# First network's batch 0 turned and routed inside the last attention steps; linear attention's input turned inside the first network

## What is computed

```python
x = L0_attn_x                                              # (4, 512, 256)
x = _layernorm(x + _L0_attn_ref(x, ...))                   # softmax attention, 16 heads of 128, causal, rope
x = _layernorm(x + _L0_ffn_ref(x, ...))                    # gated network, 688 wide, with routed low-rank terms
x = _layernorm(x + _L1_attn_ref(x, Wq, Wk, Wv, Wo, bo))    # linear attention, 32 heads of 64
x = _layernorm(x + _L1_ffn_ref(x, ...))                    # 64 experts of 176, 6 of them per token, and a shared one
```

## Time and profile before

| | |
|---|---|
| median of 3 runs | 1531.04 us (1530.15 to 1536.18) |
| the profiled execution, its own time | 1537.87 us |
| its span, first to last instruction | 1536.1 us |
| PE busy | 1414.8 us, 92% of the span |
| PE weight loads, DVE, ACT, POOL busy | 73%, 61%, 37%, 36% |
| share of the chain that ended last | PE 80%, DVE 9%, POOL 3%, ACT 2% |
| mean granted TensorE clock | 0.967 |

### The profile page before, as it was taken

How to read it: one execution, slowest core, us unless ns; L and a number is a source line. 1 busy time by engine, 2 the same in 40 slices (tenths; PEclk the granted TensorE clock), 3 DMA queues, 4 the chain that set the end, 5 groups by cost and what they waited for, 6 DMA issues and landing times.

```text
span 1536.1 us, 23836 instructions
## 1 busy us (share of the span) xinstructions
PE 1414.8 (92%) x8106; PEld 1126.1 (73%) x8106; DVE 941.8 (61%) x2170; ACT 569.5 (37%) x1441; POOL 553.4 (36%) x483
## 2 busy tenths in 40 slices
PE   7999999999999999889999799999999999766990
PEld 6777777777777777667776588788788788653650
DVE  4677777777777777744432557566665666655214
ACT  4444444444444444612121243343343333321330
POOL 3555555555555555101012223522522522204223
PEclk9999999999999999989999899999999999878996
DMA  5000000000002000110000020110200003945994
GB/s 175 1 11 1 12 0 10 0 10 0 10 0 71 0 0 1 20 62 1 1 0 1 0 76 8 47 37 15 69 7 14 7 9 85 254 153 165 274 257 123
DMA packets 68221, 76.39 MB, mean 50 GB/s; under 512 B 14205, under 2 KB 55445, under 8 KB 68149
## 3 DMA queue, kind: packets, MB, share of 16 engines
q1 hardware_dynamic: 56789, 58.49, 13.8%
q10 hardware_dynamic: 8288, 12.22, 2.6%
q0 software_dynamic: 3072, 4.72, 1.6%
HBM read 66.22 MB, written 9.21 MB: 49 GB/s over the span
## 4 chain that ended last, share of the span: by engine, by line
PE 80%; DVE 9%; POOL 3%; issue 2%; ACT 2%; DMA 2%; another core or an unknown queue 1%; POOLq 0%; ACTq 0%; DVEq 0%
PE ps L1605 37%; PE ps L1721 9%; PE ps L1706 7%; PE ps L1694 5%; PE ps L1751 4%; PE ps L1842 4%; PE ps L1699 2%; PE ps L2046 2%; PE ps L1917 1%; PE ps L2111 1%; PE ps L1907 1%; DMA sums_dram<-rows 1%; PE ps L2128 1%; PE ps L1723 1%; PE ps L1696 1%
## 5 line engine op out<-in xcount | busy, mean ns | idle before, releaser
L616 POOL TENSOR_TENSOR qk<-q,ksb 128x512 f32<-128x512 f32 x64 | 82.5, 1290 | 304.2 <-ACT q L840 214.1
L755 ACT ACTIVATE probs<-ps,nm 128x128 f32<-128x128 f32 (+3 forms) x256 | 133.8, 525 | 152.4 <-DVE nm L1115 152.4
L1721 PE MATMUL ps<-kT,qT 128*128 128x128 f32 (+3 forms) x512 | 174.6, 450 | 4.4 <-ACT probs L755 3.7
L1039 DVE TENSOR_TENSOR pT_low<-ps,pT 128x384 fp32r<-128x384 f32 (+2 forms) x256 | 99.7, 451 | 122.9 <-ACT pT L698 121.3
L1056 DVE TENSOR_TENSOR prod<-ps,rope_sb 128x1024 f32<-128x1024 f32 x128 | 150.2, 1216 | 6.4 <-PE ps L1605 6.4
L494 POOL TENSOR_TENSOR qT<-prod 64x512 f32<-64x512 f32 x64 | 81.2, 1268 | 170.2 <-DVE prod L1056 131.6
L698 ACT ACTIVATE pT<-ps 128x384 fp32r<-128x384 f32 (+2 forms) x256 | 84.9, 416 | 152.4 <-PE ps L1751 152.4
L1706 PE MATMUL ps<-U,oT 128*128 (+1 forms) x512 | 124.6, 386 | 0.7 <-ACT oT L698 0.7
L494 POOL TENSOR_TENSOR kT<-prod 64x512 f32<-64x512 f32 x64 | 81.4, 1272 | 111.6 <-DVE prod L1056 109.1
L1115 DVE TENSOR_REDUCE nm<-ps 128x1 f32<-128x128 f32 (+3 forms) x256 | 114.0, 484 | 12.1 <-PE ps L1723 12.1
L1165 DVE SCALAR_TENSOR_TENSOR acc<-ps,rinv,acc 128x256 f32<-128x256 f32 x256 | 109.6, 479 | 13.5 <-PE ps L1706 11.9
(11 more groups left out here) (256 smaller groups left out, 2746.4 us busy)
## 6 DMA issues: line engine op xcount, KB each, us to landing
eg<-in_L_ffn_w_gate_dram SPq DMA_DIRECT2D x16, 704.0 KB
eg<-in_L_ffn_w_up_dram SPq DMA_DIRECT2D x16, 704.0 KB
ed<-in_L_ffn_w_down_dram ACTq DMA_DIRECT2D x10, 640.0 KB
ksb<-ks_dram SPq DMA_DIRECT2D x16, 256.0 KB, 3.3
ed<-in_L_ffn_w_down_dram SPq DMA_DIRECT2D x6, 640.0 KB
rows_dram<-rows ACTq DMA_DIRECT2D x4, 640.0 KB, 3.9
acc<-in_L_attn_x_dram SPq DMA_DIRECT2D x4, 512.0 KB
wq_in<-in_L_attn_wq_dram SPq DMA_DIRECT2D x8, 256.0 KB, 2.8
```

The costliest lines, as they stand in the source:

```text
L616: nc.gpsimd.tensor_tensor(qk[:], q3[:], ksb[b % 2][:], ALU.mult).then_inc(qk_ready, 1)
L755: nc.scalar.activation(probs[hh][:, off:off + (i + 1) * P], ps[:, BS + i % 2, 0:(i + 1) * P], ACT.Exp, bias=nm[:, hh, i:i + 1], accum_out= ...
L1039: return nc.vector.tensor_tensor(o, whole, hi.bitcast(F32), ALU.subtract)
L1721: pe.matmul(ps[:, bank, 0:(i + 1) * P], qT[:, hh, b, i * P:(i + 1) * P], kT[:, hh, b, 0:(i + 1) * P], start=True, stop=False)
```

## The change

It does four things.

1. Batch 0 is turned in step 6 of the last pair (banks 2 and 3), its halves are made in the same step, and its router products are issued before the last `pv_and`. ACT's sigmoid and DVE's `route0(0)` come before the last `oT` copy and the last additions. Two groups of base products stand around the last `project_out`.
2. The weight pieces are split in another order: `la` third instead of last, so ACT waits for `la` in step 5 instead of step 6, and DVE makes the last three pieces in step 7.
3. In the last batch of the first network batches 0, 1 and 2 of linear attention's input are turned and split (banks 4 and 5): one after tile `m == 3`, one after the last tile, one inside the down products. `x2T` becomes one pair of buffers per batch, `wk3` a first chunk and the later three, and POOL splits the first key weights and centres the values when the last `turn_x1` is done.
4. At the seam the first four key tiles and the first queries come directly after the last products; the statistics, normalisation, turning and splitting of batch 3 come after or beside them, and the bias is added after that.

```diff
-        w0_pieces += [([h[:] for h in lb], lb_in[:]), ([h[:] for h in la], la_in[:])]
+        w0_pieces.insert(2, ([h[:] for h in la], la_in[:]))
+        w0_pieces.append(([h[:] for h in lb], lb_in[:]))
+        w0_hi_at = {4: (0, 1), 5: (2, 3, 4), 6: (5,)}
+        w0_lo_at = {5: (0, 1), 6: (2,), 7: (3, 4, 5)}
...
@@ gpsimd @@
-            pool.wait_ge(ffn_ready, TILES)
-            halve_wk3(0, lambda: root(8))
-            x2_rest(3)
-            pool.wait_ge(x2_ready, TILES)
+            pool.wait_ge(x1_turned, BATCH * KD)
+            halve_wk3(0)
+            centre_wv3(0)
+            root(8)
+            pool.wait_ge(ffn_ready, TILES)
             nc.gpsimd.memset(kvT[0][:].bitcast(F32), 0.0).then_inc(zeroed, 1)
             nc.gpsimd.memset(kvT[1][:].bitcast(F32), 0.0).then_inc(zeroed, 1)
+            x2_rest(3)
...
@@ scalar @@
+                if n == 5:
+                    act.wait_ge(la_loaded, 8 * 16)
                 if n == 6:
                     act.wait_ge(lb_loaded, 64)
-                    act.wait_ge(la_loaded, 8 * 16)
...
+                if last and n == 6:
+                    x1_halves(0)
...
-            x1_halves(0)
             scores0(0)
+            act.wait_ge(pv_done, STEPS * PAIRS)
+            copy(oT[:], ps[:, BO, :]).then_inc(ot_copied, 1)
             xa_halves(0)
...
             for p in range(PPC):
                 keys(0, p, FIRST_KEYS[p])
             grams(0, 0)
+            x2_rows(3)
+            x2_halves(3, 4)
             act.wait_ge(zeroed, 5)
...
@@ vector @@
-                    if n >= 5:
-                        for m in (2 * (n - 5), 2 * (n - 5) + 1):
+                    if n == 6:
+                        x1_rests(0)
+                    if n in w0_lo_at:
+                        for m in w0_lo_at[n]:
...
-            dve.wait_ge(acc_added, 4 * STEPS * PAIRS)
             link(nc.vector.memset(wnext[:], 1.0 / R0))
-            dve.wait_ge(x1_ready, TPB)
-            x1_rests(0)
             route0(0)
             take_weights()
+            add(STEPS * PAIRS - 1, STEPS - 1)
             xa_rests(0)
+            dve.wait_ge(acc_added, 4 * STEPS * PAIRS)
...
             for p in range(PPC):
                 keys(0, p, FIRST_KEYS[p])
+            statistics(tiles(3), 2 * BATCH)
+            norm2(3)
+            x2_rests(3, 4)

             dve.wait_ge(dn_loaded, 13 * 16)
             dve.wait_ge(x2lo_ready, BATCH)
...
@@ tensor @@
+                if n == 6 and last_pair:
+                    pe.wait_ge(products_ready, 2 * PROJECTIONS)
+                    turn_x1(0)
                 for i in range(TPB):
                     pe.wait_ge(probs_ready, 4 * s + i + 1)
...
+                    if m == 3 and last_one:
+                        turn_x2(0, 4)
                 if not last_one:
-                    first_products(b + 1, False)
+                    first_products(b + 1)
+                else:
+                    pe.wait_ge(x2Tlo_ready, KD)
+                    turn_x2(1, 4)
                 pe.wait_ge(hid_ready, b * FT0 + FT0)
                 for i in range(TPB):
+                    if last_one and i == 2:
+                        pe.wait_ge(x2Tlo_ready, 2 * KD)
+                        turn_x2(2, 4)
...
-            turn_x1(0, True)
+            pe.wait_ge(w0_lo, 3)
+            first_products(0)
+            pv_and(STEPS * PAIRS - 1, STEPS - 1)
+            pe.wait_ge(w0_lo, 5)
+            base_products(0, 0, 1)
+            project_out(STEPS * PAIRS - 1, PAIRS - 1, STEPS - 1)
+            base_products(0, 1, 1)
+            turn_xa(0)
             pe.wait_ge(w0_lo, 6)
-            first_products(0, True)
             pe.wait_ge(dn_loaded, 13 * 16)
...
-                               lambda h: wk3[h][:, bass.ds(c, 1), k, :], k == 0, k == KD - 1)
+                               lambda h: wk3_first[h][:, k, :] if at_first else wk3_later[h][:, bass.ds(c - 1, 1), k, :],
+                               k == 0, k == KD - 1)
...
-            pe.wait_ge(ffn_added, TILES)
-            for b in range(BATCH):
-                pe.wait_ge(x2_ready, b * TPB + TPB)
-                for k in range(KD):
-                    for i in range(TPB):
-                        last = pe.transpose(ps[:, 2 * b + k, i * P:(i + 1) * P],
-                                            acc[:, b * TPB + i, k * P:(k + 1) * P], ident[:])
-                    last.then_inc(x2_turned, 1)
-            pe.wait_ge(x2Tlo_ready, BATCH * KD)
             pe.wait_ge(wk3_ready, 1)
+            pe.wait_ge(x2Tlo_ready, 3 * KD)
             for p in range(PPC):
                 keys(0, 0, 0, p, FIRST_KEYS[p])
-            pe.wait_ge(x2lo_ready, BATCH)
-            pe.wait_ge(x2_ones, 2 * BATCH)
+            pe.wait_ge(ffn_added, TILES)
+            pe.wait_ge(wq3_ready, PPC)
+            queries(0, 0, 0)
+            pe.wait_ge(x2lo_ready, 1)
+            pe.wait_ge(x2_ones, 2)
             grams(0, 0)
+            turn_x2(3, 4)
             chunk3(0, True, False)
```

More of the change, by code:

```diff
@@ L737, in ffn_weights_halves, with x1_halves @@
                     act.wait_ge(proj_ready, PROJECTIONS)
+                if n == 5:
+                    act.wait_ge(la_loaded, 8 * 16)
                 if n == 6:
                     act.wait_ge(lb_loaded, 64)
-                    act.wait_ge(la_loaded, 8 * 16)
-                for halves, whole in w0_pieces[2 * (n - 4):2 * (n - 3)]:
+                for m in w0_hi_at[n]:
+                    halves, whole = w0_pieces[m]
                     copy(halves[0], whole).then_inc(w0_hi, 1)
+            def x1_halves(b):
+                for k in range(KD):
+                    act.wait_ge(x1_turned, b * KD + (k + 1))
+                    copy(x1T[b % 2][0][:, k, :], ps[:, x1_bank(b) + k, :]).then_inc(x1hi_ready, 1)
             def step(g, n, first, last):
@@ L822, in ffn0 @@
                         x1_halves(b + 1)
+                    if m == 3 and last:
+                        x2_halves(0, 4)
                 if not last:
@@ L1153, in step, with x1_rests @@
                             rest(halves[1], whole, halves[0]).then_inc(w0_lo, 1)
+            def x1_rests(b):
+                for k in range(KD):
+                    dve.wait_ge(x1hi_ready, b * KD + (k + 1))
+                    rest(x1T[b % 2][1][:, k, :], ps[:, x1_bank(b) + k, :], x1T[b % 2][0][:, k, :]).then_inc(x1lo_ready, 1)
             def add(s, n):
@@ L1188, in norm1 @@
                     link(nc.vector.tensor_scalar(a, a, meanvar[:, i, 0:1], rstd[:, i:i + 1], ALU.subtract, ALU.mult))
-            def x1_rests(b):
-                for k in range(KD):
-                    dve.wait_ge(x1hi_ready, b * KD + (k + 1))
-                    rest(x1T[b % 2][1][:, k, :], ps[:, 4 + k, :], x1T[b % 2][0][:, k, :]).then_inc(x1lo_ready, 1)
             def route0(b):
+                bank = logits_bank(b)
                 dve.wait_ge(sig_ready, b + 1)
@@ L1239, in xa_rests, with x2_rests, norm2 @@
                     dve.wait_ge(xahi_ready, b * 2 + (w + 1))
-                    rest(xaT[1][:, w, :], ps[0:NL, 4 + w, :], xaT[0][:, w, :]).then_inc(xalo_ready, 1)
+                    rest(xaT[1][:, w, :], ps[0:NL, xa_bank(b) + w, :], xaT[0][:, w, :]).then_inc(xalo_ready, 1)
+            def x2_rests(b, bank):
+                for k in range(KD):
+                    dve.wait_ge(x2Thi_ready, b * KD + (k + 1))
+                    rest(x2T[b][1][:, k, :], ps[:, bank + k, :], x2T[b][0][:, k, :]).then_inc(x2Tlo_ready, 1)
+            def norm2(b):
+                for i, a in enumerate(tiles(b)):
+                    nc.vector.tensor_scalar(a, a, meanvar[:, i, 0:1], rstd[:, i:i + 1],
+                                            ALU.subtract, ALU.mult).then_inc(x2_ready, 1)
             def ffn0(b, last):
@@ L1709, in project_out, with turn_x1 @@
                         last.then_inc(out_ready, 1)
+            def turn_x1(b):
+                pe.wait_ge(x1_ready, b * TPB + TPB)
+                if b:
+                    pe.wait_ge(xalo_ready, b * 2)
+                rows_in = x1s if b else acc
+                for k in range(KD):
+                    for i in range(TPB):
+                        last = pe.transpose(ps[:, x1_bank(b) + k, i * P:(i + 1) * P], rows_in[:, i, k * P:(k + 1) * P], ident[:])
+                    last.then_inc(x1_turned, 1)
             def step(g, n, first, last_pair):
@@ L1822, in ffn0 @@
                             pe.wait_ge(ffn_added, (b - 1) * TPB + 2 * w + m + 1)
-                        base(m, w)
-                if first:
-                    turn_xa(0)
+                        if not (first and w):
+                            base(m, w)
                 pe.wait_ge(xalo_ready, b * 2 + 2)
```

148 lines of the change are left out of this document (78 added, 70 removed).

## The result

The changed kernel takes 1515.15 us in the median of its runs (1512.38 to 1516.38), the kernel before 1532.37 us in the same group (1530.15 to 1536.18). The medians are 17.2 us apart. The measured ratio is 0.9877 with a 95% interval of 0.986 to 0.9895, which is 18.8 us (16.1 to 21.5). The forecast was 1514.5 us, 16.5 us less. In all that follows, one execution of the kernel before (2845.58 us) and one of `e3_fours` (2640.3 us) are left out of the comparisons as slow ones.

The account below looks back on a forecast made before the run. PE bounds the kernel, busy 92% of the span, so only its idle time and low clock can give time. 9.8 + 6.7 = 16.5 us off the median of 1531.04 gave 1514.5 us, range 1509 to 1522.

Parts of the forecast that it names:

- seam 1, what goes: From the last `pv_and` to the third low-rank group: five PE waits, low clock and turning go, 12.3 us.
- (a): Step 6 of attention: eight transposes now ahead of that step's own transposes, all on the path, cost 1.0 us.
- (b): Step 6 of attention: DVE makes two `x1T` rests instead of two `gu` pieces, about 0.2 us later.
- (c): ACT waits for `la` in step 5, so step 6's exponentials start 1.3 us later; bounds 0 and 2.
- seam 1: Attention into the first network, 656 to 680 us: net gain of 9.8 us.
- three turns in batch 3: Last batch of the first network: 3.2 us more PE work, 1.75 us of clock back, net +0.3 us.
- bias with POOL's `qk` beside it: Start of linear attention: DVE's four additions, 4.62 us, plus 1.3 for one `qk`; bounds 0 and 1.3.
- stop before the second key tile: Start of linear attention: PE stands still for some 7 us from 873 while DVE adds the bias.
- low clock behind it: First key tiles after PE's stop run at a lower clock, costing 2.5 us; bounds 1.2 and 4.
- seam 2: First network into linear attention, 836 to 890 us: 9.2 us less 2.5 of low clock, gain 6.7 us.
- the filled gap: One turn fills the 1.41 us before the down products, so their clock stays high: 1.75 us back.
- Rival 4: Linear attention's loop: PE works out an address per matmul, so the kernel is slower, 1541 at 140 ns each; chance 0.03.

Follow-up runs that it names:

- e3_fours: The changed kernel with GpSimd's 16 expert gathers issued in fours, each later four behind further groups' gate and up products; 0.9904 of the kernel before.
- e3_turn_twice: The changed kernel with the eight transposes of batch 0's turn in step 6 done twice into the same banks; 0.9879 of the kernel before.
- e2_bias_la: The changed kernel with the bias additions moved out of the stop at linear attention's start and `la` loaded ahead of `lb`; 0.9819 of the kernel before.
- e2_turn_in_down: The changed kernel with the turn of `x2`'s batch 1 moved from ahead of the down products to behind their first tile; 0.991 of the kernel before.

## Why the prediction was right, point by point

| term, us | predicted | rows after |
|---|---|---|
| seam 1, what goes | 12.3 | 13.8 |
| turn in step 6 (a) | 1.0 | 0.25 |
| DVE in step 6 (b) | 0.2 | about 0.15 |
| wait for `la` (c) | 1.3 | 0.8 |
| seam 1 | 9.8 | 12.6 |
| three turns in batch 3 | +0.3 | 0 |
| bias with POOL's `qk` beside it | 5.9 | 5.60 |
| stop before the second key tile | some 7 | 7.25 |
| low clock behind it | 2.5 | 2.75 |
| seam 2 | 6.7 | 7.4 |
| both | 16.5 | 20.0 |
| time, difference of medians | 16.5 | 17.2 (15.0 and 18.7 in two other groups) |

**Seam 1, what goes.** Every one of the five idle times went, and `turn_xa` waits for nothing. What went is the 12.6 gained and the 1.2 by which step 7's scores came later than they should. The 0.7 us taken off for overlapping records should have stayed in; the other 0.8 I can't place.

**(a)** was mis-sized by four. It priced the transposes by their length and forgot that they could stand in a wait that was there; `e3_turn_twice` shows the full 0.88 us as soon as that wait is used up. **(c)** had the right mechanism and place. Its own terms (633.6 + 0.4 + 1.45) give 635.45 and 1.1 us, not 635.6 and 1.3, and the copies behind the wait were added with their full lengths, though their rows overlap; the exponentials came 0.8 us late, and 0.8 us is what `e2_bias_la` gets back.

**Seam 2** went by its steps: keys at the full clock behind the last product, bias behind `x2_rest(3)`, its additions stretched to 5.60 us. The rule of the Trainium skill that the prediction weighed (SBUF — State Buffer, "Who interferes with whom") had been entered as a whole `qk` of 1.3 us; the trace shows 1.0 over the 4.62 of the earlier trace rows. It agrees with the rule: the `qk` started 0.16 us ahead of the bias and had 1.1 us left. The path to the bias was rounded up by 0.15 us (870.9 + 2.35 is 873.25, not 873.4). The down products lost their low clock as forecast, but `e2_turn_in_down` has the gap back without it, so the reason given, the filled gap, isn't shown.

**Between the seams and after.** Rival 4, the loop's addresses, fell at once: keys out of `wk_later` take 387 ns at the least and 393 in the median as in the earlier trace rows. In linear attention the distance of 20.6 us doesn't change by more than 0.3.

**Why 20.0 in the rows and 17.2 in the time.** The prediction noted that the profiled execution was 6.8 us above the median and said that neither seam was known to hold the difference. That was the weak step: seam 1 seems to have held much of it. Of the 6.1 us of low clock, 4.6 were absent in another execution of the same instructions, and the first half alone measures 8.8 us. That the forecast met the time to 0.7 us is partly luck: seam 1's other terms, together 2.8 us too small a gain, stood against a clock term that was large for the usual execution. How often the clock falls that long at seam 1 isn't shown, since the record has only the mean clock of the executions without a profile. Open too is the half of the second seam: 2.6 us measured where the rows say 7.4, and both halves give 11.4 where the whole gives 15.0 in the same group (their intervals, some 2 us either way for each, still meet). Its own trace places it 8.1 us ahead at seam 2, so the rest is lost elsewhere. The median of its granted clocks, 0.969, is not above the 0.970 of the kernel before, though less of the seam is at the low clock; its profile has the longest remote waits but one, 15.1 us, and a short low clock at 981 us that cost 1.6. Which of these is the rule for this kernel wasn't tried.

## What to carry to other kernels

Read a low-clock term from more than one execution before it enters a sum; the idle times repeated within 0.04 us, and the clock behind them did not at the first seam (the mean clock of each execution tells how far one profile stands from the rest). Price a moved instruction by the wait into which it is moved, not by its length, and look at what else is released together with the work that is next late: here moving four additions out of the second seam was worth 7.9 us, as much as the rows give for that seam's whole rearrangement (7.4). And a transfer moved out of a quiet stretch into a busy one has a new landing time.

## What the runs showed of the hardware

A stop of TensorE went with a row of indirect gathers from GpSimd: with twelve of them held back by 7.8 us the long stop moved too (it began 8 to 9 us behind the first gather of the row in both cases, and 12 to 13 us behind it in three other kernels), with TensorE's stream shifted by 127 waits it stayed, and with at most four gathers in a row it was gone. Which resource they share isn't shown, and a row of gathers isn't enough: one profile of the changed kernel had all 16 and no stop.

A wait of TensorE on a semaphore that was already there took between 35 and 73 ns (127 of them moved its first transposes from 4.86 to 9.31 us).

A DVE addition of two SBUF tensors of 128x1024, 1.22 us long elsewhere, took 2.20 us when a GpSimd product with 1.1 us left to run lay beside its start.

Four gathers took 3.0 us from their last issue to their use at a DMA share of 0.39, and 8.4 and 7.7 us among the weight loads, at 1.06.

Behind the same stops (1.06, 1.73 and 1.56 us; 1.02, 1.74 and 1.57) TensorE's granted clock was 0.73 on average over 656 to 680 us in one execution and 0.93 in another, that is, some 13 and 3 us of it at 1.2 GHz.
